# A decoder layer in fp32: attention split in two halves that run one batch apart

## What is computed

```python
x = x + attn(layernorm(x))        # RWKV-4: k, v, r = projections of token-shift mixes; wkv recurrence;
                                  # layernorm(wkv) * sigmoid(r), projected by Wo
x = x + wkv2(k=layernorm(x), v=ctx)          # second recurrence with its own decay w, bonus u
x = x + (silu(h @ gate.T * gs) * (h @ up.T * us)) @ down.T * ds    # h = layernorm(x), 1408 inner
```

## Time and profile before

| | us |
|---|---|
| median of 3 runs | 614.09 |
| profiled execution | 616.2 |
| its span, first to last instruction | 614.2 |
| attention of batch 0, up to the first `up0` | 130.6 |
| the three loop rounds | 138.3, 137.0, 138.7 |
| the last feed-forward, with the store | 69.7 |
| busy: PE, DVE, ACT, POOL | 539.0, 460.5, 345.0, 47.9 |

### The profile page before, as it was taken

How to read it: one execution, slowest core, us unless ns; L and a number is a source line. 1 busy time by engine, 2 the same in 40 slices (tenths; PEclk the granted TensorE clock), 3 DMA queues, 4 the chain that set the end, 5 groups by cost and what they waited for, 6 DMA issues and landing times.

```text
span 614.2 us, 8078 instructions
## 1 busy us (share of the span) xinstructions
PE 539.0 (88%) x2658; PEld 384.2 (63%) x2658; DVE 460.5 (75%) x727; ACT 345.0 (56%) x546; POOL 47.9 (8%) x155
## 2 busy tenths in 40 slices
PE   3998671269999997999999997999999997999995
PEld 2443331168447577997447477996447487999994
DVE  5899429928999459978999469968998479863343
ACT  4648447548546455758546365768556365763231
POOL 2000110012001110012001010012001010010000
PEclk9999695569999999999999998999999998999999
DMA  8999300010010000020020000030010000000001
GB/s 308 378 379 375 117 0 0 1 40 31 0 69 1 1 0 2 35 86 17 0 68 0 0 0 0 34 99 3 0 68 0 0 0 0 34 35 1 1 34 37
DMA packets 11877, 34.65 MB, mean 56 GB/s; under 512 B 912, under 2 KB 912, under 8 KB 11664
## 3 DMA queue, kind: packets, MB, share of 16 engines
...
...
## 4 chain that ended last, share of the span: by engine, by line
PE 71%; DVE 12%; issue 6%; ACT 5%; POOL 2%; DMA 2%; SPq 0%; DVEq 0%; POOLq 0%; ACTq 0%
PE bank L473 27%; PE gu L557 19%; PE dacc L487 10%; PE bank L533 8%; PE bank L462 5%; DVE t_slot L773 2%; DMA t_xres<-in_x 2%; PE bank L510 1%; DVE t_stats L752 1%; DVE t_z L765 1%; POOL t_rstd L439 1%; ACT t_z L626 1%; DVE t_st L900 1%; ACT L580 1%; DVE t_slot L881 1%
## 5 line engine op out<-in xcount | busy, mean ns | idle before, releaser
L557 PE MATMUL gu<-t_z4h,t_gate 128*128 128x256 f32 x352 | 92.5, 294 | 15.0 <-DVE t_h L931 13.2
L557 PE MATMUL gu<-t_z4l,t_gate 128*128 128x256 f32 x352 | 90.5, 289 | 0.0
L557 PE MATMUL gu<-t_z4h,t_up 128*128 128x256 f32 x352 | 90.1, 288 | 0.0
L557 PE MATMUL gu<-t_z4l,t_up 128*128 128x256 f32 x352 | 89.9, 287 | 0.0
L557 PEld LDWEIGHTS gu<-t_z4h,t_gate 128*128 128x128 f32 x352 | 69.0, 196 | 19.1 <-DVE t_h L931 14.8
L697 ACT ACTIVATE t_h<-gu,t_fsc 128x256 f32<-128x256 f32 x88 | 40.2, 472 | 66.6 <-PE gu L557 62.1
L487 PE MATMUL dacc<-t_down,t_hh 128*128 128x512 f32 x176 | 73.3, 416 | 0.0
L557 PEld LDWEIGHTS gu<-t_z4l,t_gate 128*128 128x128 f32 x352 | 69.1, 196 | 0.9
L487 PE MATMUL dacc<-t_down,t_hl 128*128 128x512 f32 x176 | 69.5, 395 | 0.0
L557 PEld LDWEIGHTS gu<-t_z4h,t_up 128*128 128x128 f32 x352 | 68.9, 196 | 0.0
L557 PEld LDWEIGHTS gu<-t_z4l,t_up 128*128 128x128 f32 x352 | 68.8, 195 | 0.0
...
## 6 DMA issues: line engine op xcount, KB each, us to landing
...
```

What stands on the lines that cost most here:

```text
L557: last = pe.matmul(gu[u % 2][:, side, :], as_read(w[:, k, i * P:(i + 1) * P], exact), as_read(part[:, k, hf * HALF:(hf + 1) * HALF], exact ...
```

## The change

Attention is cut behind the first recurrence. The loop runs over b = 1 and 2 only: in a round stand the first half of batch b+1, the second half of batch b and the feed-forward of batch b-1. `*_FIRST` now holds both halves of batch 0 and the first half of batch 1 (its steps end in "+"). A new list, `*_NEXT`, holds the second half of batch 3 and the feed-forward of batch 2; `*_LAST` is the feed-forward of batch 3 as before, in a new order. All lists are reordered. `fin2+` and `fin3+` stand behind `z4_0_*` in `DVE_FIRST`.

The buffers follow: x is loaded twice, once into `mixv` for the first half (it is normalised in place there and waits for `nv3` of the batch before) and once into `xres` for the residual; `ctx` comes in four loads a batch through a new two-block tile; `mixr` of a batch lies in `z`, `xf` or `mixk`; `rw` writes `tanh_r`; the maximum and the gap of `front` lie in `slot`, so `front` of block c+2 waits for `fin` of block c, and issues one small memset more; the second recurrence writes `z`; the first normalisation has statistics and semaphores of its own. `return2` and `turn1` are waited for as a whole by their ACT readers. The load of `up` and of `down` move behind other steps of SP's list. Waits for PSUM banks and slots are worked out from the four lists (`placed`, `need_earlier`).

```diff
-    LATE = ("xf_2", "xf_3", "nb7", "sq7", "rn7", "norm7", "turn4_1", "z4_1_0", "z4_1_1")
+    LATE = ("nb7", "sq7", "rn7", "norm7", "turn4_1", "z4_1_0", "z4_1_1")
     PE_FIRST = """
...
+        turn1 k0 k1 v0 v1 k2 k3 v2 v3 r0 r1 r2 r3 turn2 return2 turn1+ k0+ k1+ v0+ wo v1+ turn3 r0+ r1+
+        r2+ r3+ y k2+ k3+ v2+ v3+ turn4_0 flag
         """.split()
     PE_BODY = """
...
+        up0 up1 turn4_1 up2 turn2 up3 up4 up5 return2 down0 up6 down1 turn1 up7 wo k0 k1 v0 k2 k3 down2
+        v1 down3 down4 up8 up9 down5 v2 v3 up10 up11 down6 down7 up12 up13 down8 down9 down10 turn3 up14
+        up15 down11 r0 up16 up17 up18 down12 down13 r1 up19 r2 r3 down14 down15 up20 down16 up21 down17
+        y down18 down19 down20 down21 turn4_0
+        """.split()
+
+    PE_NEXT = """
+        up0 up1 turn4_1 up2 turn2 up3 up4 up5 return2 down0 down1 wo up6 up7 turn3 up8 down2 up9 down3
+        up10 up11 down4 down5 down6 down7 up12 up13 down8 down9 down10 up14 up15 down11 up16 up17 up18
+        up19 down12 down13 down14 up20 up21 y down15 down16 down17 down18 down19 turn4_0 down20 down21
         """.split()
     PE_LAST = """
...
+        up0 up1 up2 up3 up4 up5 down0 down1 down2 up6 up7 turn4_1 down3 up8 up9 up10 down4 down5 down6
+        up11 up12 down7 down8 down9 down10 up13 up14 up15 up16 down11 down12 down13 down14 down15 up17
+        up18 up19 up20 up21 down16 down17 down18 down19 down20 down21
         """.split()
     ACT_FIRST = """
         norm0 norm1 share_k0 share_k1 share_k2 share_k3 share_v0 share_v1 share_v2 share_v3 share_r0
...
+        share_r1 front0 share_r2 front1 share_r3 part0 part1 front2 front3 tanh0 tanh1 tanh2 part2 part3
+        tanh3 weigh0 weigh1 norm2 norm3 norm0+ rw0 rw1 rw2 rw3 norm1+ share_k0+ share_k1+ share_k2+
+        share_k3+ share_v0+ share_v1+ share_v2+ share_v3+ share_r0+ share_r1+ share_r2+ share_r3+
+        front0+ front1+ part0+ sq4 norm4 sq5 norm5 xfront0 part1+ xfront1 xpart0 xfront2 xpart1 tanh0+
+        tanh1+ tanh2+ xfront3 xpart2 tanh3+ xpart3 weigh2 sq6 weigh3 front2+ front3+ weigh4 norm6 weigh5
+        part2+ z4_0_0 z4_0_1 part3+ flag
         """.split()
     ACT_BODY = """
...
+        sq7 silu0 norm7 z4_1_0 z4_1_1 silu1 silu2 high0 silu3 norm2 high1 norm3 silu4 silu5 rw0 rw1
+        norm0 rw2 rw3 norm1 share_k0 share_k1 share_k2 share_k3 share_v0 high2 silu6 silu7 share_v1
+        share_v2 share_v3 front0 front1 part0 share_r0 share_r1 sq4 share_r2 share_r3 sq5 high3 norm4
+        norm5 part1 silu8 silu9 front2 front3 high4 silu10 silu11 silu12 high5 silu13 part2 part3 silu14
+        silu15 high6 xfront0 high7 xfront1 silu16 silu17 xpart0 high8 xpart1 xfront2 xfront3 silu18
+        silu19 tanh0 tanh1 tanh2 tanh3 xpart2 high9 xpart3 silu20 silu21 high10 sq6 norm6 z4_0_0 z4_0_1
+        """.split()
+
+    ACT_NEXT = """
+        sq7 norm7 silu0 silu1 z4_1_0 z4_1_1 silu2 high0 silu3 high1 norm2 norm3 rw0 rw1 rw2 rw3 silu4
+        sq4 silu5 norm4 high2 sq5 silu6 silu7 norm5 xfront0 xfront1 silu8 silu9 xpart0 high3 silu10
+        high4 silu11 xpart1 high5 silu12 silu13 xfront2 xfront3 silu14 high6 silu15 high7 silu16 silu17
+        silu18 silu19 xpart2 xpart3 high8 silu20 silu21 high9 sq6 high10 norm6 z4_0_0 z4_0_1
         """.split()
     ACT_LAST = """
...
+        silu0 silu1 silu2 high0 silu3 high1 sq7 silu4 silu5 high2 norm7 silu6 silu7 high3 silu8 silu9
+        z4_1_0 z4_1_1 high4 silu10 silu11 silu12 high5 silu13 high6 silu14 silu15 high7 silu16 silu17
+        high8 silu18 silu19 silu20 high9 silu21 high10
         """.split()
     DVE_FIRST = """
...
+        stat1_0 stat1_1 norm0 norm1 mixk0 mixk1 mixk2 mixk3 mixv0 mixv1 mixv2 mixv3 mixr0 front0 front1
+        nv0 mixr1 mixr2 nv1 den0 num0 part0 den1 num1 mixr3 part1 fin0 front2 fin1 front3 nv2 den2 num2
+        nv3 part2 den3 num3 part3 fin2 fin3 stat2_0 stat2_1 norm2 norm3 stat1_0+ stat1_1+ norm0+ rw0 rw1
+        rw2 norm1+ mixk0+ mixk1+ mixk2+ mixk3+ mixv0+ mixv1+ mixv2+ mixv3+ front0+ rw3 front1+ den0+
+        mixr0+ mixr1+ mixr2+ mixr3+ nv0+ num0+ part0+ den1+ x1_0 x1_1 x1_2 x1_3 fin0+ norm4 nv1+ norm5
+        num1+ xfront0 part1+ xin0 xden0 fin1+ xnum0 xfront1 xpart0 xin1 xden1 xfin0 xnum1 xfront2 xpart1
+        xden2 xin2 xfin1 xnum2 xfront3 xpart2 xin3 xden3 xnum3 xpart3 xfin2 xfin3 xf_0 xf_1 xf_2 xf_3
+        front2+ norm6 front3+ den2+ nv2+ num2+ part2+ nv3+ den3+ num3+ weigh part3+ flag z4_0_0 z4_0_1
+        fin2+ fin3+
         """.split()
     DVE_BODY = """
...
+        norm7 prod0 z4_1_0 z4_1_1 prod1 prod2 rest0 stat2_0 stat2_1 prod3 norm2 norm3 stat1_0 prod4
+        prod5 stat1_1 rw0 rw1 norm0 rw2 norm1 mixk0 mixk1 rest1 mixk2 rw3 mixk3 mixv0 mixv1 mixv2 mixv3
+        x1_0 x1_1 x1_2 x1_3 front0 rest2 front1 den0 nv0 num0 prod6 prod7 part0 den1 mixr0 mixr1 fin0
+        mixr2 nv1 mixr3 num1 norm4 part1 front2 fin1 prod8 prod9 front3 rest3 nv2 den2 num2 prod10
+        prod11 part2 rest4 den3 nv3 prod12 num3 rest5 prod13 norm5 part3 out0 fin2 out1 xfront0 prod14
+        prod15 fin3 xfront1 rest6 xin0 xden0 xnum0 prod16 xpart0 xin1 xden1 xnum1 prod17 xpart1 xfin0
+        xfront2 xfin1 xfront3 rest7 rest8 xin2 xden2 xnum2 prod18 xpart2 xin3 xden3 xnum3 prod19 xpart3
+        rest9 xfin2 xfin3 prod20 prod21 xf_0 xf_1 rest10 out2 norm6 xf_2 out3 z4_0_0 xf_3 z4_0_1
+        """.split()
+
+    DVE_NEXT = """
+        norm7 prod0 z4_1_0 z4_1_1 prod1 prod2 stat2_0 stat2_1 prod3 rest0 norm2 norm3 rw0 rw1 rw2 rw3
+        prod4 x1_0 x1_1 prod5 norm4 x1_2 rest1 rest2 x1_3 norm5 prod6 prod7 xfront0 xfront1 xin0 xden0
+        xnum0 xin1 prod8 prod9 xpart0 xden1 xnum1 rest3 xpart1 prod10 prod11 xfin0 rest4 xfront2 rest5
+        xfin1 prod12 prod13 xfront3 out0 out1 xin2 prod14 prod15 xden2 rest6 xnum2 prod16 rest7 prod17
+        xpart2 xden3 prod18 xin3 xnum3 prod19 xpart3 xfin2 xfin3 rest8 xf_0 xf_1 rest9 prod20 prod21
+        norm6 rest10 z4_0_0 z4_0_1 out2 out3 xf_2 xf_3
         """.split()
...
     POOL_FIRST = """
...
+        rn0 rn1 rn2 rn3 rn0+ rn1+ nb4 rn4 nb5 rn5 nb6 rn6
         """.split()
     POOL_BODY = """
...
+        nb7 rn7 rn2 rn3 rn0 rn1 nb4 rn4 nb5 rn5 nb6 rn6
+        """.split()
+
+    POOL_NEXT = """
+        nb7 rn7 rn2 rn3 nb4 rn4 nb5 rn5 nb6 rn6
         """.split()
     POOL_LAST = """
     SP_FIRST = """
...
+        words1 xload0+ xload1+ words2 ctx2 ctx3
         """.split()
     SP_BODY = """
...
+        ctx0 ctx1 rload0 rload1 xload0 xload1 ctx2 ctx3 out0 out1 out2 out3
+        """.split()
+
+    SP_NEXT = """
+        ctx0 rload0 rload1 ctx1 ctx2 ctx3 out0 out1 out2 out3
         """.split()
 ...
+    AHEAD = ("stat1_", "share_k", "share_v", "share_r", "mixk", "mixv", "mixr", "k", "v", "r", "front", "den", "nv",
+             "num", "part", "fin", "tanh", "xload")
+    AHEAD_ONE = ("rn0", "rn1", "norm0", "norm1", "turn1")
+
+    def lead(s):
+
+        if s in LATE or kind(s) in FFN_KINDS:
+            return -1
+        return int(kind(s) in AHEAD or s in AHEAD_ONE)
+
...
+        ctxt = sb("ctxt", 2, T)
-        ctxt = mixv
...
         def run_rest(eng, step, orders):
 
-            with eng.Fori(1, B) as b:
+            with eng.Fori(1, B - 1) as b:
                 for s in orders[1]:
                     if s in LATE:
                         step(s, b - 1, None)
                     elif kind(s) in FFN_KINDS:
                         step(s, None, b - 1)
+                    elif lead(s):
+                        step(s, b + 1, None)
                     else:
                         step(s, b, None)
             for s in orders[2]:
                 if s in LATE:
+                    step(s, B - 2, None)
+                elif kind(s) in FFN_KINDS:
+                    step(s, None, B - 2)
+                else:
+                    step(s, B - 1, None)
+            for s in orders[3]:
+                if s in LATE:
                     step(s, B - 1, None)
                 else:
                     step(s, None, B - 1)
...
              def load_x(b, hf):
 
 
+                need(sp, newv_done, b - 1, C)
+                sp.dma_start(mixv[:, hf * HB:(hf + 1) * HB, :], rows_of(b, hf)).then_inc(x_in[hf], 16)
+
+            def load_res(b, hf):
+
+
                 need(sp, xf_done, b - 1, (hf + 1) * HB)
-                src = x[b, :, :] if isinstance(b, int) else x[bass.ds(b, 1), :, :].rearrange("a t d -> (a t) d")
-                sp.dma_start(xres[:, hf * HB:(hf + 1) * HB, :],
-                             src[hf * HALF:(hf + 1) * HALF, :].rearrange("(n p) d -> p n d", p=P)).then_inc(x_in[hf], 16)
-
-            def load_ctx(b):
-
-                need_filled(sp, b, "v", C - 1)
+                sp.dma_start(xres[:, hf * HB:(hf + 1) * HB, :], rows_of(b, hf)).then_inc(res_in[hf], 16)
+
+            def load_ctx(b, c):
+
+
+                need(sp, inp_done, b - 1, C + c - 1)
                 src = ctx_t[b, :, :] if isinstance(b, int) else ctx_t[bass.ds(b, 1), :, :].rearrange("a d t -> (a d) t")
```

(30 more changed lines are left out.)

371 lines of the change are left out of this document (218 added, 153 removed).

## The result

The changed kernel took 598.88 us (median; runs from 598.28 to 599.37) against 614.03 of the kernel before in the same comparison: 0.9745 times, 95% interval 0.9731 to 0.976. The forecast was 596.4 in a range of 583 to 611.

A forecast was written before the change was run, and what follows sets the result against it. PE bounds the rounds; the first stage wastes some 60 us, the change's target. 165 + 136.8 + 135.5 + 89.5 + 69.7 = 596.5, less 0.1 for median against span: 596.4 us, range 583 to 611.

The forecast's parts named there:

- First stage: Up to the first `up0`, with batch 1's first half interleaved: 165 us, walked from the lists, between bounds 149.2 and 183.
- First round: First of the two loop rounds: 136.8 us, which is 135.5 plus 1.3 taken from the kernel before.
- second: Second loop round: `up0` at 134.2 by the boundary's chain, plus 1.3 of other waits: 135.5 us; bounds 130 and 140.
- Fourth stage: New list after the rounds, without projections and `turn1`: 86.8 us plus 2.7 of waits, 89.5; bounds 87 and 97.
- Tail: Feed-forward of batch 3 at the kernel's end: 69.7 us, as before.
- From the span to the time: Profiled span of the kernel before, 614.2, is 0.1 above the median 614.09, so the summed 596.5 becomes 596.4 us.
- The mark at the boundary: Sign to look for: PE's longest wait in a round at the boundary, behind `turn4_0`, released by DVE's `z4`.
- Rival 1: DVE bounds the rounds, its steps taking listed lengths instead of overlapped starts: 610 us, still faster; chance 0.17.
- Rival 2: Slow PE clock throughout the first stage doubles 41.4 us of work: 634 us, slower; decides from 43%; chance 0.06.
- Rival 3: Banks and lists serialise the two halves of the first stage: 614 us, no change; chance 0.05.
- P: Length of the first stage, until the first `up0`: 165 us forecast.
- Rival 4: Tighter schedule than walked: first stage 155, rounds 131, fourth stage 87.5; 574 us at the extreme, 582 halfway; chance 0.12.

## Why the prediction was right

The mechanism held, and all five terms lie within 2 us. Span against span it was 596.5 against 596.4, and that it came so near is luck, since the errors cancel:

- **First stage**, 165 forecast, 165.31 measured. The walk of the lists was right to about a microsecond at each mark: `front0+` 84 (84.79), `wo` 91 to 105 (89.9 to 103.8), `turn3` ended near 111 (110.6), `xfin3` 142 (141.9), `v3+` 158 (158.3), the last `z4` 164.6 (165.1). Walking the order, rather than halving between the bounds of 149 and 183 or 187, was the choice that counted. x for batch 1 was issued at 51.86 and cost nothing, as said.
- **First round** 136.8 (136.72), **second** 135.5 (136.63). The 7.6 us from `nb6` to `up0` taken from the first stage of before was 8.65 here (293.38 to 302.03): there DVE had no `out2` and `out3` in the way, and with `norm6` ahead of them it is 7.60 again, as the experiment on the order showed. `y` ended 126.7 us into the round, and 126.5 by the sum (125.2 and the 1.3 of waits, which measured 0.7 + 0.5). But two errors meet in that number. The sum of a round has no term for the low clock behind the boundary, which took 1.9 us here, though it had taken 1.8 out of the round of before. And PE's work without waits and low clock was 128.8 us (136.72 less 6.05 of waits and 1.9), not 129.9. That the first round was hit and the second missed is luck too: the 1.3 that the first got on top, taken over from the kernel before, did not come, for the two rounds measured alike, and it stood in for DVE's queue.
- **Fourth stage** 89.5 (87.55). The 2.7 us of waits at `return2` and `turn3` did not come; one wait of 0.57 did. Nothing in DVE's shorter list held them up.
- **Tail** 69.7 (70.19).
- **From the span to the time.** The one step that was wrong in kind. Both profiled executions lie 1.9 to 2.0 us above their span; I set the span of before beside the median of before, which matched to 0.1 only because that profiled execution (616.2) was a long one. The changed kernel's (598.28) was its shortest. Those 2.5 us are the whole miss: 596.4 against 598.88. The median less the forecast difference of spans, 614.09 - 17.7, is the same 596.4, so the better reading is that a single profiled execution stands for the median only within the spread of the runs, here 611 to 617 for the kernel before.

**The mark at the boundary** was right as far as it went. PE's longest waits in a round are there, ahead of `turn4_0` and behind it, and DVE's `z4` releases the longer one, as said. I derived them from the chain of the normalisation, and that chain is 7.6 us of the 8.65. What I left out is the order of DVE's list, with `out2` and `out3` ahead of what PE needs: 1.06 us.

**Rival 1**, DVE as the bound, gave 610 and was the right worry: the slack I worked out as 1.3 us is none (0.5 of wait ahead of `y`; a lighter DVE gave 0.8 a round), and 2.26 us more of DVE's work in each round, with as much in the first stage, gave 612. It did not happen because DVE's steps ran at the overlapped starts, as taken.

**Rival 2**, the slow clock. The granted clock of the first stage was 0.73, 1.00, 0.89 and 0.87 behind 61.4: PE regained 2.4 GHz within its bursts. The eight sets of `k` and `v` and `wo` on the way took 1.7 us more than at the full clock, where I had charged 2.2 in one place. The share from which this rival decides was wrong in my sum: with the 4 us that it counts as charged it is 21.7/41.4, 52% of that work, and not 43%. The rule of the Trainium skill ("TensorE: Matmul & The Clock Gate", "HAM oscillation — how this bites in real kernels"), bursts with waits between them drop to the slow clock again and again, shows at the boundaries of the rounds, at 0.50 behind 4.6 us of waiting, and costs 1.9 us each time there instead of 41 in the first stage.

**Rival 3**, no overlap in the first stage, I priced at P = 183 and 614. The experiment that made it so gave 195.8 and 629: the batches one after the other don't fit end to end (134 and 62 us), since the first half of batch 1 alone waits in itself, 6.8 us at `turn1+` and 4.0 at a `v`. It would have been slower than before, by 2.3%, and belonged on the other side.

**Rival 4**, a tighter schedule, came true for the fourth stage alone (87.55, where it had 87.5); the first stage and the rounds stayed 10 and 6 us above it. Halfway between its 574 and the forecast is 585, not 582.
